# Token transformer kernel: interpolation in four column tiles, a twelve-row convolution, probabilities and queries moved by DMA, loop unrolled

## What is computed (the reference, cut)

```
h = leaky_relu(batchnorm(conv2d(x, stem_w, 4)))          # 96 x 21 x 21
offset = conv2d(h, off_w, 4)                             # 32 x 5 x 5
sampled = bilinear samples of h at 16 taps x 25 positions, moved by offset
h = leaky_relu(batchnorm(einsum(sampled, dcn_w)))        # 25 tokens x 192
h = concat([h, txt])                                     # 102 tokens
h = h + attention(layernorm(h))                          # 12 heads of 16, int8 activations,
                                                         # probabilities are powers of two
h = h + gelu(layernorm(h) @ in_w + in_b) @ out_w         # hidden 768
```

## Time and profile before

| | |
|---|---|
| median of three runs | 1175.64 us (1172.16 to 1175.76) |
| time of the profiled execution | 1170.16 us |
| its span (first to last instruction) | 1168.4 us |
| mean granted TensorE clock | 0.927 of full speed |
| TensorE matmul busy | 991.8 us (85%) |
| VectorE busy | 998.8 us (85%) |
| ScalarE busy | 868.9 us (74%) |
| GpSimd busy | 274.5 us (23%) |

### The profile page before, as it was taken

The page is one execution under the profiler, slowest core; times in us unless marked ns, Lnnn a source line. Parts: engine busy times, 40 slices in busy tenths (PEclk is TensorE's granted clock), DMA queues, the critical chain, the costliest instruction groups (busy, mean ns, idle before and its releaser), DMA issues. The chain is left out here.

```text
span 1168.4 us, 21251 instructions
## 1 busy us (share of the span) xinstructions
PE 991.8 (85%) x6306; PEld 604.7 (52%) x6306; DVE 998.8 (85%) x2187; ACT 868.9 (74%) x1969; POOL 274.5 (23%) x241
## 2 busy tenths in 40 slices
PE   2668779898989989898998989898989989897756
PEld 1234445646464655546464555546464655555344
DVE  2777889898999899898889999899989998997760
ACT  1324778879695979789596969789796969786662
POOL 4011212323231213223231223123231322121210
PEclk9877889989998999989899989999899989989768
DMA  6000000010101010010101000010101000101000
GB/s 169 17 14 23 3 13 24 14 35 14 34 14 34 4 28 16 14 33 13 33 13 33 13 22 11 13 33 13 33 13 34 14 22 2 36 1 36 1 11 11
DMA packets 29481, 26.79 MB, mean 23 GB/s; under 512 B 3655, under 2 KB 28398, under 8 KB 29326
## 3 DMA queue, kind: packets, MB, share of 16 engines
q1 hardware_dynamic: 29422, 26.07, 8.1%
HBM read 19.82 MB, written 6.24 MB: 22 GB/s over the span
## 5 line engine op out<-in xcount | busy, mean ns | idle before, releaser
L542 POOL TENSOR_TENSOR m_sb<-mx_sb,a_sb 128x1020 f16<-128x1020 f16 x64 | 143.0, 2235 | 487.2 <-DVE mx_sb L955 487.2
L1138 PE MATMUL bank<-hats_sb,ht_sb 126*96 126x400 f32 (+1 forms) x512 | 212.9, 550 | 15.0 <-DVE hats_sb L861 12.7
L678 ACT ACTIVATE ee_sb<-ee_sb,rs_sb 128x102 f32<-128x102 f32 x640 | 180.1, 383 | 1.3 <-DVE rs_sb L1011 1.3
L1264 PE MATMUL bank<-w_out_sb,ge_sb 128*102 128x192 f32 x768 | 140.2, 333 | 7.2 <-DVE y_sb L1052 3.2
L1138 PEld LDWEIGHTS bank<-hats_sb,ht_sb 126*96 126x96 f32 (+1 forms) x512 | 78.5, 173 | 127.2 <-issue 107.4
L1264 PEld LDWEIGHTS bank<-w_out_sb,ge_sb 128*102 128x102 f32 x768 | 122.6, 170 | 20.9 <-issue 16.8
L861 DVE TENSOR_TENSOR hats_sb<-hats_sb 126x1600 f32<-126x1600 f32 x64 | 116.5, 1820 | 0.1
L604 ACT ACTIVATE hats_sb<-bank 126x400 f32<-126x400 f32 x256 | 107.9, 519 | 0.6 <-PE bank L1129 0.6
L998 DVE SCALAR_TENSOR_TENSOR ee_sb<-sq_sb,sc_sb,ep_sb 128x1020 f32<-128x1020 f32 x64 | 81.6, 1275 | 24.4 <-ACT sq_sb L671 24.2
L625 ACT ACTIVATE xt_sb<-bank 128x204 f32<-128x204 f32 x128 | 44.6, 349 | 63.7 <-PE bank L1161 62.4
L1151 PE MATMUL bank<-wdcn_sb,samp_sb 96*100 96x192 f32 (+1 forms) x512 | 88.4, 332 | 0.5 <-ACT samp_sb L613 0.5
(11 more groups left out here) (163 smaller groups left out, 1963.9 us busy)
## 6 DMA issues: line engine op xcount, KB each, us to landing
xc_sb<-x_col SPq DMA_DIRECT2D x32, 165.4 KB, 2.9
out<-y_sb SPq DMA_DIRECT2D x32, 153.0 KB
xa_sb<-txt SPq DMA_DIRECT2D x16, 231.0 KB
xr_sb<-txt SPq DMA_DIRECT2D x16, 231.0 KB
tok_scratch<-tokb_sb SPq DMA_DIRECT2D x16, 75.0 KB
xa_sb<-tok_scratch SPq DMA_DIRECT2D x16, 75.0 KB
xr_sb<-tok_scratch SPq DMA_DIRECT2D x16, 75.0 KB
wdcn_sb<-dcn_w SPq DMA_DIRECT2D x1, 1152.0 KB
```

What stands on the lines that cost most here:

```text
L542: nc.gpsimd.tensor_tensor(M16[b][:], MX[b][:].unsqueeze(2).to_broadcast([128, RT, TOK]), A16[b][:], ALU.subtract).then_inc(m_done, 1)
L678: last = nc.scalar.activation(EE[b][:, r, :], EE[b][:, r, :], ACT.Ln, scale=RS[b][:, r:r + 1])
L1138: last = mm(bank[t.banks[0]][0:C1, 0:SMP], HT[0:rows, t.i, j, :], HATS[b][0:rows, 1 + j, :], start=(j == 0), stop=(j == NCH - 1))
L1264: last = mm(bank[t.banks[0]][0:TOK, 0:D], GE[:, f, t.i * TOK:(t.i + 1) * TOK], WOUT[:, f, :], start=(f == 0), stop=(f == FT - 1))
```

## The change

- **Interpolation.** The same four pixel chunks, but as column tiles of 32 array columns. In tiles 0 to 2 the three thirds of the channels are computed for the first 12 taps (300 columns); in tile 3 the last four taps (100 columns) of the three thirds, one after the other. Per image 24 matmuls instead of 4. The PSUM tile becomes 128x300.
- **Convolution.** 12 matmuls over 128 rows and one of a single row (ones by bias) in place of 16 over 96 rows. The weight is loaded in that layout (7 loads for 4).
- **Leaky ReLU.** ScalarE's Prelu writes `H` and `TOKB` straight from PSUM; VectorE's STEM and DCN stages and the tiles `LK`, `LKD` are gone.
- **Probabilities.** `P` is padded to 128 columns per block; SyncE issues one transposing DMA per image (stage PT) from `P` to `PT`, now two buffers. TensorE's ten transposes and ScalarE's two copies are gone. PW of an image waits for the transposing DMA of the image two earlier.
- **Queries.** Twelve DMAs on SyncE per group (stage QD) copy `QB` into `Q0`, `Q1`; the twelve VectorE multiplications are gone. SC waits for them.
- **Order.** `SLOT` and `BANKS` are new: every engine has a new order. SyncE's turn is LA, LR, PT (second, third, fourth image), QD, YO0, LX, YO1, PT (first image), DCN. The loop is unrolled: all waits are against constants.

```diff
+PACKED = TAPS * C1 // 128
+REST = TAPS - PACKED
...
-    with engine.Fori(0, TURNS) as turn:
-        for slot in range(LOOP_FROM, LOOP_FROM + GRP):
-            run_slot(name, slot, stages, turn)
-    loop_end()
-    for slot in range(LOOP_TO, LAST_SLOT + 1):
+    for slot in range(FIRST_SLOT, LAST_SLOT + 1):
         run_slot(name, slot, stages)
...
+            def place_queries(t):
+
+                sp.wait_ge(qb_done, t.count(1, 1))
+                if t.n < 1:
+                    sp.wait_ge(fill_s, FILLS)
+                else:
+                    sp.wait_ge(score_full, t.count(GRP, 0))
+                for h in range(NH):
+                    dst, block, at = (Q0, 0, h * TOK) if h < FIRST_HEADS else (Q1, 1, h * TOK - 128 * CROSS)
+                    rows = slice(h % FIRST_HEADS * HD, h % FIRST_HEADS * HD + HD)
+                    sp.dma_start(dst[rows, :, at:at + TOK],
+                                 QB[rows, block, :].rearrange("p (g q) -> p g q", q=TOK)).then_inc(q_in, 16)
+
+            def turn_probs(t):
+
+                b = t.i % 2
+                sp.wait_ge(p_done, t.count(1, 1))
+                if t.n >= 2:
+                    sp.wait_ge(pv_full, t.count(1, -1))
+                sp.dma_start_transpose(PT[b][:], P[b][:].rearrange("p r k -> p (r k)")).then_inc(pt_in[b], 16)
...
+                nc.scalar.activation(H[:, t.i, 0:NPIX], bank[BANKS[f"STEM{t.i // 2}"][t.i % 2]][0:C1, 0:NPIX], ACT.Prelu,
+                                     alpha=SLOPE).then_inc(h_done, 1)
...
+                nc.scalar.activation(TOKB[:], bank[t.banks[0]][0:GRP * POS, 0:D], ACT.Prelu,
+                                     alpha=SLOPE).then_inc(tok_done, 1)
...
-                for h in range(NH):
-                    dst, rows, block, at = (Q0, 128, 0, h * TOK) if h < FIRST_HEADS else (Q1, 64, 1, h * TOK - 128 * CROSS)
-                    own_h = h % FIRST_HEADS
-                    last = v.tensor_scalar(dst[:, :, at:at + TOK], QB[0:rows, block, :].rearrange("p (g q) -> p g q", q=TOK),
-                                           own[0:rows, own_h:own_h + 1], None, ALU.mult)
-                last.then_inc(qk_done, 1)
...
                 if t.n >= 2:
-                    dve.wait_ge(pt_full, t.count(2, -2))
-                v.tensor_scalar(P[b][:].rearrange("p h k -> p (h k)"), RR[:], RATIO_GAIN, None, ALU.mult).then_inc(pw_done, 1)
+                    dve.wait_ge(pt_in[b], t.count(8, 0 if b == 0 else -8))
+                v.tensor_scalar(P[b][:, :, 0:TOK], RR[:].rearrange("p (h k) -> p h k", k=TOK), RATIO_GAIN, None, ALU.mult).then_inc(pw_done, 1)
...
                 for j in range(NCH):
-                    rows = CH if j < NCH - 1 else LAST
-                    last = mm(bank[t.banks[0]][0:C1, 0:SMP], HT[0:rows, t.i, j, :], HATS[b][0:rows, 1 + j, :],
-                              start=(j == 0), stop=(j == NCH - 1))
+                    rows = slice(0, CH if j < NCH - 1 else LAST)
+                    for c in range(C1 // 32):
+                        mm(out[32 * c:32 * c + 32, 0:PACKED * POS], HT[rows, t.i, j, 32 * c:32 * c + 32],
+                           HATS[b][rows, 1 + j, 0:PACKED * POS], start=(j == 0), stop=(j == NCH - 1))
+                    for k in range(3 * j, 3 * j + 3):
+                        c, i = divmod(k, NCH)
+                        rest = slice(0, CH if i < NCH - 1 else LAST)
+                        last = mm(out[C1:128, c * REST * POS:(c + 1) * REST * POS], HT[rest, t.i, i, 32 * c:32 * c + 32],
+                                  HATS[b][rest, 1 + i, PACKED * POS:SMP], start=(i == 0), stop=(i == NCH - 1))
                 last.then_inc(samp_full, 1)
...
-                for k in range(TAPS):
-                    rows = slice(0, C1 + 1 if k == 0 else C1)
-                    last = mm(dst, SAMP[rows, k, :, :].rearrange("c g p -> c (g p)"), WD[rows, k, :],
-                              start=(k == 0), stop=(k == TAPS - 1))
+                mm(dst, onesq[0:1, 0:GRP * POS], dcnb[:], start=True, stop=False)
+                for k in range(PACKED):
+                    last = mm(dst, SAMP[:, k, :, :].rearrange("c g p -> c (g p)"), WD[:, k, :],
+                              start=False, stop=(k == PACKED - 1))
...
-            def transpose_p(t):
...
+                pe.wait_ge(pt_in[b], t.count(8, 16 if b == 0 else 8))
```

More of the change, by code:

```diff
@@ L123, in take @@
         if b in self.last:
-            before, at, by, looped = self.last[b]
-            if t.turn is not None:
-                self.pe.wait_ge(before, t.turn * by + at)
-            else:
-                if looped:
-                    at += by * (TURNS - 1)
-                self.pe.wait_ge(before, at)
-        self.last[b] = (drained, value, step, t.turn is not None)
-    def check(self):
-        for b, (before, at, by, _) in self.entered.items():
-            drained, value, step, _ = self.last[b]
-            assert drained is before and value == at + by and step == by, b
+            before, at = self.last[b]
@@ L153, in of_group, with run_slot @@
     def of_group(self, per=1, plus=0):
-        value = per * (self.n // GRP) + plus
-        return value if self.turn is None else self.turn * per + value
-def run_slot(engine, slot, stages, turn=None):
+        return per * (self.n // GRP) + plus
+def run_slot(engine, slot, stages):
     for of_engine, stage, lag in PHASES[slot % GRP]:
@@ L187, in assert_apart, with walk @@
         assert not any(start < place(engine, stage, n) < end for n in range(2 * IMG)), stage
-def walk(engine, name, stages, loop_end=lambda: None):
+def walk(engine, name, stages):
     assert {stage for part in PHASES for e, stage, _ in part if e == name} == set(stages)
@@ L277, in build @@
         XC = sb("xc", [SROWS, 2, NPIX])
-        LK = [sb(f"lk{b}", [C1, NPIX]) for b in range(2)]
         H = sb("h", [C1, GRP, NCH * CH])
@@ L463, in load_residual @@
             def load_residual(t):
[L464 removed]
+                n = t.count(GRP)
                 if t.n >= 1:
```

250 lines of the change are left out of this document (98 added, 152 removed).

## The result

The changed kernel takes 1188.24 us (median of four runs, 1182.69 to 1194.15), the kernel before 1173.90 us beside it on the same chip: a ratio of 1.013, 95% interval 1.009 to 1.017. It is slower, by 1.3%. The profiled execution took 1189.12 us.

What follows compares the result with a forecast made beforehand. VectorE and TensorE were taken as both close to the bound. VectorE's relief gave 57.8 us, plus 1.0 and 0.5 for transfers: 59.3 us a turn, 87 us less over fifteen, +3 us tail; median 1092 us, range 1058 to 1163.

Steps and rivals of the forecast that it cites:

- VectorE's 7.3 us: VectorE's query multiplications, two maxima and one wait go: 7.3 us off the 65.1 us turn, giving 57.8.
- with the other 2.3 us of waits kept: VectorE's period after relief, 57.8 us, still includes 2.3 us of its former 3.9 us of waits a turn.
- The tiles run side by side: Interpolation's four float32 column tiles on TensorE overlap, as bf16 ones do: 2.3 us an image.
- L1111's rate: The only float32 matmuls in four column tiles, 16 in 1.57 us; slowness put down to their four-pixel operand step.
- The good end: Interpolation tiles overlap: 2.3 us an image, 3.0 us less a turn; TensorE then needs 52.2 us without waits.
- limit of 3.5: Stated failure sign: the prediction fails if interpolation takes over 3.5 us per image.
- the bad end: Interpolation tiles as slow as L1111: 4.7 us an image, 6.8 us more a turn; TensorE needs 62.0 us.
- slower than before: Rival, chance 0.11: slow transposing DMAs stall VectorE's PW; at 14 us each, a turn 3.5 us longer, 1231 us.
- by 1 to 3 us: Query copies, 6.3 to 7.9 us, fit under VectorE's work before the scores with this margin; 0.5 us a turn allowed.
- TensorE's slack: TensorE's spare time in a turn, 57.8 - 52.2 us, said to cover one slow-clock stretch after waiting for queries.
- Column tiles as slow as L1111: Rival, chance 0.12: TensorE becomes the bound at 62.0 us plus waits, 63 to 64 us a turn, 1147 to 1162 us.
- SyncE's order: Rival, chance 0.20: token store, load and second transposing transfer queue serially, costing 4 us a turn, about 1129 us.

Runs made afterwards that it cites:

- e4: Kernel before, unrolled, plus only ScalarE's Prelu in place of VectorE's two maxima: 1164.3 us, ratio 0.992 to the kernel before.
- e1: Changed kernel with the last pixel chunk of interpolation over all 126 rows (zeros beyond the last pixel) instead of 63: 1138.8 us, ratio 0.970.
- e15: e7 plus six thrown-away matmuls a turn in TensorE's wait before the scores: 1115.4 us, ratio 0.949.
- e16: e1 plus two thrown-away matmuls a turn in TensorE's wait before the scores: 1121.6 us, ratio 0.953.
- e2: Kernel before with its loop unrolled and nothing else: 1171.6 us, ratio 0.999 to the kernel before.
- e11: e1 with the last six of a turn's twelve query copies issued by GpSimd instead of SyncE: 1099.0 us, ratio 0.933.
- e9: Changed kernel with interpolation matmuls reordered so the row count changes three times an image in place of seven, 63-row records kept: 1159.6 us, ratio 0.987.
- e8: e7 with the last six of a turn's twelve query copies issued by GpSimd instead of SyncE: 1097.3 us, ratio 0.935.
- e7: e1 with PSUM banks renamed for the convolution and the first projection of values: 1146.6 us, ratio 0.978.
- e3: Kernel before, unrolled, in its old order, plus only the column tiles (63-row last chunk) and the twelve-row convolution: 1171.8 us, ratio 0.997.

## Why the prediction was wrong

- **What bounds the kernel.** Right that a change must relieve both engines. Wrong in the use of it: I subtracted VectorE's 7.3 us from the period as if it were alone, "with the other 2.3 us of waits kept". In e4 4.3 us a turn were taken off and the period moved by 0.2 us. What VectorE lost in its maxima came back as waits for ScalarE and as longer instructions.
- **Interpolation.** This is the step that failed first. "The tiles run side by side" is right, and so is the rate: 2.19 us in e1 for a forecast of 2.3. The operand's step as the cause of L1111's rate is borne out in so far as four float32 tiles without a step run at full rate; no run gave these tiles a step. But both ends were worked out from columns alone, and neither had the row count of the last chunk in it, though the code names it (`LAST`). The good end carries over the rate of the untiled records, which have one short chunk at the end, to an order that changes the row count seven times. The image took 4.03 us, 0.5 us past the limit of 3.5 at which I had said the prediction fails. The error is 1.73 x 4 = 6.9 us a turn.
- **TensorE's need.** Forecast 52.2 us a turn without waits. Measured 604 / (650 / 66.9) = 62.2 us, by chance the bad end of 62.0. Of the 10.0 us between, 6.9 are the interpolation and 1.5 the stem's serial pairs (its busy time went from 37.8 to 62.1 us in 16 turns), which I had not looked for in `BANKS`. The remaining 1.6 us I have not split. On top come waits of 45.8 / (650 / 66.9) = 4.7 us a turn: 62.2 + 4.7 = 66.9.
- **VectorE's need.** 551 / (650 / 66.9) = 56.7 us of work a turn. By the same measure it was 602 / (650 / 65.1) = 60.3 before, and 5.8 us were taken off: 54.5. The 2.2 us between are operations that run slower in the changed kernel. The largest is `gq_sb`, 505 ns before and 838 ns after, 1.3 us a turn; others went the other way. Of the strided `P`, which I had put at nothing, the in-place operation went from 415 to 542 ns, 0.5 us a turn; whether by the gaps in `P` or by its place isn't separated. The two groups in after (by form; busy us, mean ns, idle before):

```profile
L928 DVE TENSOR_SCALAR gq_sb<-qq_sb,sc_sb 128x1020 f16<-128x1020 int16 x64 | 53.7, 838 | 1.6
...
L979 DVE TENSOR_SCALAR p_sb<-p_sb 128x1020 uint16<-128x1020 uint16 x64 | 34.7, 542 | 1.1
```
- **The transposing DMAs.** Right, and the rival "slower than before" did not come for its reason. They land in 3.5 us (forecast 5); TensorE waits for them 1.4 us in the whole window, and no wait of VectorE names them.
- **The query DMAs.** The mechanism was named, with its clock, but its size was off twice. An issue takes 0.64 to 0.73 us in after, not 0.28 to 0.42, so the path from cast to scores is about 8 us of issuing and 1.5 to 2 us of landing against a cover that I had fitting "by 1 to 3 us". And that TensorE's slack covers such a stretch at 1.2 GHz did not hold once the tiles were mended: in e15 and e16 the stretch behind the scores goes in all or most turns without a shorter path, for 31 and 17 us. In the changed kernel as it stands no turn between 300 and 950 us has that stretch.
- **Unrolling.** Right: 0.999 in e2.
- **The rivals.** "Column tiles as slow as L1111" came nearest, with TensorE as the bound at 62 us, but by another mechanism (the row count, not the operand). Its price of 1147 to 1162 us had 1 to 2 us of TensorE's waits a turn, where the window has 4.7. "SyncE's order" is right in place (its queue), wrong in the stage: it is the copies, not the token store.
- **The forecast itself.** The loss against before is all in the period: 15 x 1.8 = 27 us more, 10 us less before the first cast (91.1 for 101.3 us) and 2 us more of tail make 1170.2 into the 1189 us of the profiled execution. With the two faults mended (e11: full rows, copies on two queues) the change gives 1099.0 us, 0.6% over the forecast of 1092. That is partly luck: the period is 61.4 us, not 59.3, and the filling before the first turn is 13 us shorter (88.1 against 101.3 us), which I had not counted; the tail is 0.8 us shorter, where I had 3 us more.

These are the page rows of after for the two transfers (KB each, us from issue to landing), beside the earlier trace rows:

```profile
pt_sb<-p_sb SPq DMA_TRANSPOSE x64, 3.5
...
q_sb<-qb_sb SPq DMA_DIRECT2D x192, 12.8 KB, 1.9
```

## What to carry to other kernels

Before packing matmuls into column tiles, look at the row counts of all of them: pad a short chunk with zero rows, so that the row count never changes inside the packed stretch. Count small DMAs by what their issue takes on the queue, and lay them on two queues where an engine waits for the last. And where TensorE must wait a microsecond or two before a long stretch, try to fill the wait with matmuls that are thrown away, just as many as fit (too many cost more here than they gave); a period that doesn't fall when TensorE's work falls should be read together with the granted clock.

## What the runs showed of the hardware

- Each change between 63 and 126 stationary rows among column tiles costs 0.16 to 0.40 us by its place (e1, e9); 63-row records alone run at the rate of 126-row ones.
- Four float32 column tiles run side by side: 300 columns in each of three and three records of 100 in the fourth in 0.25 us, no more than 300 columns of one untiled record at 0.94 ns each.
- An SBUF-to-SBUF copy of 12.8 KB takes about 0.7 us to issue on SyncE (8.22 and 8.73 us for twelve; 4.80 for six in e8) and 0.5 us on GpSimd (3.10 us for six), and the two queues run at once.
- A wait of 2.9 us on TensorE was followed by 1.2 GHz for the stretch behind the scores (e7), and two matmuls in a wait of 0.8 us were worth 17 us over 16 turns (e16). More work on TensorE cost nothing in e3 (clock 1.00 for 0.96), and less gained nothing in e7 (0.92 for e1's 0.93, with the wait for the queries longer).
- A transposing DMA of 320 KB within SBUF lands in 3.5 us.
